# Batches of token products, lane marks shared out between engines, clearing in pieces, and a count that moves ahead of the last products

## The reference

```python
# layer 1: self-attention over the 1024 positions of an image
energy = einsum('bmi,bmj->bij', Wq @ x, Wk @ x)
y      = einsum('bcj,bij->bci', Wv @ x, softmax(energy))
x      = alpha * y + x
# layer 2: 16 proxies, a causal running sum over the tokens
prods = einsum('pd,bsd->bps', proxy, x)
y     = cumsum(prods[..., None] * x[:, None], axis=2)
out   = einsum('bps,bpsd->bsd', softmax(prods / 4, axis=1), y)
# layer 3: 8 experts, each token goes to the best two
top_w, top_idx = softmax(top_k(flat @ gate_w.T, 2))
out = sum_e combine[:, e] * (gelu(flat @ w1[e] + b1[e]) @ w2[e] + b2[e])
```

## Time and profile before

| | us |
|---|---|
| median of three runs | 832.53 (831.14 to 834.49) |
| profiled execution | 832.61 |
| its span, first to last instruction | 830.9 |
| stage A, B, C in that span | 241, 142, 448 |
| TensorE busy in A, B, C | 206, 84, 431 |

### The profile page before, as it was taken

The page is one execution under the profiler, slowest core; times in us unless marked ns, Lnnn a source line. Parts: engine busy times, 40 slices in busy tenths (PEclk is TensorE's granted clock), DMA queues, the critical chain, the costliest instruction groups (busy, mean ns, idle before and its releaser), DMA issues.

```text
span 830.9 us, 18535 instructions
## 1 busy us (share of the span) xinstructions
PE 721.0 (87%) x5410; PEld 682.9 (82%) x5411; DVE 503.1 (61%) x1152; ACT 310.9 (37%) x599; POOL 399.7 (48%) x462
## 2 busy tenths in 40 slices
PE   5898998989558667634999999999999999999993
PEld 4797897978546555424999999999999999999993
DVE  3787787877665989972545544554455445544551
ACT  2664854736324434212323332333223322332230
POOL 1564563734944323225355555555555555555233
PEclk9999999999968989855999999999999999999997
DMA  7569476493351212122175653754565445544222
GB/s 263 197 224 416 155 275 246 174 399 140 148 225 56 97 59 102 53 78 60 27 249 154 179 193 62 239 158 141 179 209 157 140 145 152 146 140 145 27 27 28
DMA packets 45868, 130.08 MB, mean 157 GB/s; under 512 B 5184, under 2 KB 35520, under 8 KB 41216
## 3 DMA queue, kind: packets, MB, share of 16 engines
q1 hardware_dynamic: 30560, 104.86, 33.4%
q0 software_dynamic: 13904, 19.45, 13.5%
q10 hardware_dynamic: 1360, 5.24, 1.6%
HBM read 186.80 MB, written 47.59 MB: 282 GB/s over the span
## 4 chain that ended last, share of the span: by engine, by line
PE 51%; issue 1%; DMA 1%; POOL 1%; DVE 0%; POOLq 0%; ACT 0%; DVEq 0%
PE ps_h L73 9%; PE ps_h L74 8%; PE ps_h L75 8%; PE ps_y L73 8%; PE ps_y L75 8%; PE ps_y L74 8%; PE ps_x L1545 2%; DMA out_tok<-y,to_row 0%; POOL out_tok L1425 0%; DMA x_rows<-normed,from_row 0%; POOLq L1348 0%; DVE yb L1505 0%; DVE xtl L1485 0%; DVE y L1512 0%; ACT xth L1450 0%
## 5 line engine op out<-in xcount | busy, mean ns | idle before, releaser
L1459 ACT ACTIVATE g<-ps_h,bias 128x256 f32<-128x256 f32 x288 | 120.8, 471 | 278.8 <-PE ps_h L75 278.8
L1425 POOL DMA_INDIRECT out_tok<-y,to_row x72 | 118.5, 1645 | 160.4 <-DVE y L1512 148.6
L73 PE MATMUL ps_h<-xth,wbuf 128*128 128x256 f32 x576 | 164.3, 285 | 3.3 <-issue 1.8
L73 PE MATMUL ps_y<-wbuf,gl 128*128 x576 | 164.5, 286 | 0.0
L74 PE MATMUL ps_h<-xtl,wbuf 128*128 128x256 f32 x576 | 164.1, 285 | 0.0
L75 PE MATMUL ps_h<-xth,wbuf 128*128 128x256 f32 x576 | 162.8, 283 | 0.0
L75 PE MATMUL ps_y<-wbuf,gh 128*128 x576 | 161.5, 280 | 0.0
L74 PE MATMUL ps_y<-wbuf,gh 128*128 x576 | 161.5, 280 | 0.0
L73 PEld LDWEIGHTS ps_h<-xth,wbuf 128*128 128x128 f32 x576 | 109.2, 190 | 3.9 <-issue 2.1
L75 PEld LDWEIGHTS ps_h<-xth,wbuf 128*128 128x128 f32 x576 | 110.8, 192 | 0.0
L74 PEld LDWEIGHTS ps_h<-xtl,wbuf 128*128 128x128 f32 x576 | 109.5, 190 | 0.0
(11 more groups left out here) (235 smaller groups left out, 1369.5 us busy)
## 6 DMA issues: line engine op xcount, KB each, us to landing
wbuf<-wsplit SPq DMA_DIRECT2D x71, 2048.0 KB, 7.3
wsplit<-wbuf SPq DMA_DIRECT2D x14, 2048.0 KB, 12.0
wraw<-in_w SPq DMA_DIRECT2D x16, 1024.0 KB, 7.6
raw<-in_x_ch ACTq DMA_DIRECT2D x5, 1024.0 KB, 10.1
normed<-x SPq DMA_DIRECT2D x8, 528.0 KB, 3.1
tok<-in_x_tok SPq DMA_DIRECT2D x1, 4096.0 KB, 16.6
out_tok<-tok SPq DMA_DIRECT2D x8, 512.0 KB, 3.7
x_rows<-normed,from_row POOLq DMA_INDIRECT x72, 3.2
```

The lines of the kernel that those rows point to most:

```text
L73: eng.matmul(out, ll, rh, start=first, stop=False)
L1425: pool.indirect_dma_start(out=out, out_offset=bass.IndirectOffsetOnAxis(ap=to_row[:, par, s:s + 1], axis=0), in_=y[:, par, s, :], in_offse ...
L1459: last = act.activation(g[:, f, :], ps_h[:, q, f % 2, :], ACT.Gelu_apprx_tanh, bias=bias1[:, bass.ds(e, 1), f:f + 1].rearrange("p a f -> p ...
```

## The change

1. The batches of token tiles become 16, 8, 4 and 4. The loop of stage A runs over two images, and images 2 and 3 are written out. In image 2 GpSimd makes the products of the first 16 tiles behind its second low part, VectorE does the first softmax half, and ScalarE the exponential at the image's end. In image 3 follow the batches of 8 and 4.
2. At the start of stage B, `prod` and `weight_t` are cleared in halves, TensorE's transposes wait for the two copies they read (`turn_in`) and not for all of `prepare`, and ScalarE evacuates the first transposes ahead of the first normalisation.
3. `mark_cells` makes one one-hot lane vector per pair (`lane`, eight instructions), and then the cells. GpSimd multiplies all eight with the tile's number in one instruction at the end of its body (`lanes_by_tile`), and ScalarE with the token's number in one (`lanes_by_part`). `record` waits for both and for the cells; the next chunk's lane marks wait until both have read `lane`.
4. The count of the experts' tokens stands ahead of the last chunk's record.

```diff
-BATCHES = ((0, NT - IT), (NT - IT, NT - REST), (NT - REST, NT))
+BATCHES = ((0, NT - 2 * IT), (NT - 2 * IT, NT - IT), (NT - IT, NT - REST), (NT - REST, NT))
+LAST = len(BATCHES) - 1
...
-            with eng.Fori(0, B - 1) as b:
+            with eng.Fori(0, B - 2) as b:
                 image(b, True)
+            image(B - 2, True)
             image(B - 1, False)
...
                                            wbuf[:, par, at:at + n].bitcast(F32), ALU.subtract).then_inc(w_lo, 1)
+                        if more and isinstance(b, int) and (par, part) == (0, 1):
+                            tok.products(pool, fixed, *BATCHES[0], 0)
                         if not more and par == 0:
-                            tok.products(pool, fixed, *BATCHES[part], part)
+                            tok.products(pool, fixed, *BATCHES[1 + part], 1 + part)
...
                         exp_tile(it + 2)
-                    if not more and it in (REST + 1, IT - 2):
-                        n = it // (IT - 2)
+                    if not more and it in (REST, IT - 2):
+                        n = 1 + it // (IT - 2)
                         tok.exponential(act, *BATCHES[n], n)
...
                     whole_qk(b + 1, 1)
+                if isinstance(b, int) and b == B - 2:
+                    tok.exponential(act, *BATCHES[0], 0)
...
-                    if it < B - 1:
-                        tok.mean_var(dve, it * IT, (it + 1) * IT, 0, it == B - 2)
-                    if it == REST:
+                    if more and it < 2:
+                        tok.mean_var(dve, it * IT, (it + 1) * IT, 0, it == 1)
+                    if more and it == IT - 2:
+                        tok.softmax_in(dve, *BATCHES[0], 0)
+                    if not more and it == 0:
                         tok.mean_var(dve, *BATCHES[1], 1)
-                        tok.softmax_in(dve, *BATCHES[0], 0)
-                    if it == IT - 2:
                         tok.softmax_out(dve, *BATCHES[0], 0)
+                    if not more and it == REST - 1:
                         tok.softmax_in(dve, *BATCHES[1], 1)
-                    if it == IT - 1:
+                    if not more and it == REST:
+                        tok.mean_var(dve, *BATCHES[2], 2)
+                    if not more and it == REST + 1:
                         tok.softmax_out(dve, *BATCHES[1], 1)
+                    if not more and it == IT - 2:
+                        tok.softmax_in(dve, *BATCHES[2], 2)
+                    if not more and it == IT - 1:
+                        tok.softmax_out(dve, *BATCHES[2], 2)
...
                 if isinstance(c, int):
-                    pool.wait_ge(tok.weights_d, 2 if c < REST else 3)
+                    pool.wait_ge(tok.weights_d, LAST if c < REST else LAST + 1)
                 else:
-                    pool.wait_ge(tok.weights_d, 3)
+                    pool.wait_ge(tok.weights_d, LAST + 1)
                 prods = chunk_of(tok.t[:, :, :], c)[:, :, C:C + NP]
                 pool.tensor_copy(prod_in[:, :, 0:NP], prods)
-                pool.tensor_copy(weight_in[:, :, 0:NP], chunk_of(tok.weights[:, :, :], c))
+                pool.tensor_copy(weight_in[:, :, 0:NP], chunk_of(tok.weights[:, :, :], c)).then_inc(turn_in, 1)
+                if isinstance(c, int) and c == 0:
+                    pool.wait_ge(zeroed, 1)
                 pool.tensor_copy(prod[:, par].rearrange("p (b n) -> p b n", b=B)[:, :, 0:NP], prods)
...
-            def next_tile(c):
-                wait_apart(pool, lane_d, done(c))
+            def lanes_by_tile(c, par):
+
+                pool.wait_ge(lane_d, done(c))
+                pool.wait_ge(rec_mm, done(c - 2))
+                pool.tensor_tensor(lane_tile[:, par].rearrange("p (k b) l -> p k b l", k=2),
+                                   lane[:, :, :].rearrange("p (k b) l -> p k b l", k=2),
+                                   tile_no[:, :].unsqueeze(1).unsqueeze(3).to_broadcast([P, 2, B, P]), ALU.mult).then_inc(lane_tile_d, 1)
+                wait_apart(pool, lane_tile_d, done(c))
                 pool.tensor_scalar(tile_no[:, :], tile_no[:, :], 1.0, None, ALU.add).then_inc(tile_d, 1)
+                wait_apart(pool, tile_d, done(c))
...
                 if exists(i - 1):
-                    next_tile(i - 1)
+                    lanes_by_tile(i - 1, 1 - par)
...
             pool.wait_ge(const0, 1)
-            pool.wait_ge(zeroed, 1)
             body(-2, 0)
+            pool.wait_ge(zeroed, 3)
             pool.memset(causal[:, :], 1.0).then_inc(const0, 1)
...
             pool.wait_ge(routing_set, 2)
-            tok.products(pool, fixed, *BATCHES[2], 2)
+            tok.products(pool, fixed, *BATCHES[LAST], LAST)
             for i in range(-1, 2):
...
         def _(act):
-            for s in (turned_d, x1_d, gexp_d, x2_d):
+            for s in (turned_d, x1_d, gexp_d, x2_d, lane_part_d):
                 act.sem_inc(s, CREDIT)
...
                     last = act.activation(weight_t[rows, par, b, :], ps_turn[rows, P:2 * P], ACT.Copy)
                 last.then_inc(turned_d, 1)
+
+            def lanes_by_part(c, par):
+
+                act.wait_ge(lane_d, done(c))
+                act.wait_ge(rec_mm, done(c - 2))
+                act.activation(lane_part[:, par], lane[:, :, :], ACT.Copy, scale=part_id[:, 0:1]).then_inc(lane_part_d, 1)
             def body(i, par):
...
                     evacuate_turned(i + 2, par)
+                if exists(i - 1):
+                    lanes_by_part(i - 1, 1 - par)
             act.wait_ge(zeroed, 2)
-            body(-2, 0)
+            evacuate_turned(0, 0)
+            first_norm(0, 0)
+            act.wait_ge(zeroed, 3)
             body(-1, 1)
-            tok.exponential(act, *BATCHES[2], 2)
+            tok.exponential(act, *BATCHES[LAST], LAST)
             for i in range(0, 2):
...
                 dve.wait_ge(spot_d, done(c))
+                dve.wait_ge(lane_tile_d, done(c - 1))
+                dve.wait_ge(lane_part_d, done(c - 1))
+                for kb in range(KB):
+                    last = dve.tensor_scalar(lane[:, kb, :], lane_id[:, :], spot[:, 0, kb:kb + 1], None, ALU.is_equal)
+                last.then_inc(lane_d, 1)
                 dve.wait_ge(rec_mm, done(c - 2))
...
                 last.then_inc(cell_d, 1)
-                wait_apart(dve, tile_d, done(c - 1))
-                for k in range(2):
-                    for b in range(B):
-                        mine = spot[:, 0, k * B + b:k * B + b + 1]
-                        dve.tensor_scalar(lane_tile[:, par, k * B + b, :], lane_id[:, :], mine, tile_no[:, b:b + 1],
-                                          ALU.is_equal, ALU.mult)
-                        last = dve.tensor_scalar(lane_part[:, par, k * B + b, :], lane_id[:, :], mine, part_id[:, 0:1],
-                                                 ALU.is_equal, ALU.mult)
-                last.then_inc(lane_d, 1)
+
             def mark(c, par):
...
-            dve.memset(prod[:, :, :], 0.0)
-            dve.memset(weight_t[:, :, :, :], 0.0).then_inc(zeroed, 1)
+            dve.memset(prod[:, 0], 0.0).then_inc(zeroed, 1)
+            dve.memset(weight_t[:, 0], 0.0).then_inc(zeroed, 1)
+            dve.memset(prod[:, 1], 0.0)
+            dve.memset(weight_t[:, 1], 0.0)
             dve.memset(state[:, :, :], 0.0)
...
             dve.memset(nothing[:, :], 0.0).then_inc(zeroed, 1)
-            tok.mean_var(dve, *BATCHES[2], 2)
+            tok.mean_var(dve, *BATCHES[LAST], LAST)
             dve.wait_ge(routing_set, 2)
             body(-1, 1)
-            tok.softmax_in(dve, *BATCHES[2], 2)
+            tok.softmax_in(dve, *BATCHES[LAST], LAST)
             body(0, 0)
-            tok.softmax_out(dve, *BATCHES[2], 2)
+            tok.softmax_out(dve, *BATCHES[LAST], LAST)
             body(1, 1)
...
             def turn(c):
-                pe.wait_ge(prep_d, done(c))
+                pe.wait_ge(turn_in, done(c))
                 pe.wait_ge(turned_d, done(c - 1))
                 if exists(c - 3):
...
                 pe.wait_ge(x1_d, done(c))
                 pe.wait_ge(state_d, done(c - 1))
+                pe.wait_ge(prep_d, done(c))
                 for b in range(B):
                     at = b * STRIDE - b * 2 * NP
...
-                pe.wait_ge(lane_d, done(c))
+                pe.wait_ge(lane_tile_d, done(c))
+                pe.wait_ge(lane_part_d, done(c))
                 pe.wait_ge(cell_d, done(c))
...
                     rank_choices(i - 1, 1 - par)
+                if isinstance(i, int) and i == CH + 1:
+                    pe.wait_ge(count_d, done(CH - 1))
+                    pe.wait_ge(attn_d, done(CH - 1))
+                    pe.matmul(ps_count, ones[:, :], counts_m[:, :], start=True, stop=True).then_inc(counted, 1)
                 if exists(i - 2):
...
-            pe.wait_ge(zeroed, 2)
-            pe.matmul(ps_rec[:, :], nothing[:, 0:P], nothing[:, :], start=True, stop=False)
             for i in range(-2, 2):
```

(6 more changed lines are left out.)

12 lines of the change are left out of this document (6 added, 6 removed).

## The result

| | us |
|---|---|
| before, median of 20 runs | 832.51 (830.9 to 834.84) |
| changed, median of 20 runs | 826.99 (824.5 to 833.09) |
| ratio | 0.9943, 95% interval 0.9925 to 0.9961 |
| profiled execution of the changed kernel, its span | 828.92, 827.1 |

By the medians the kernel became 5.5 us faster (4.7 by the ratio), where 13.1 were forecast. The time lies inside the forecast's whole range (808 to 828) and outside its own (814 to 825); the gain is less than half of the one forecast. Its runs also spread over 8.6 us, those of before over 3.9.

The account below looks back on a forecast made before the run. Bound by stage A's chain from statistics to TensorE, stage B's mask-to-record chain, then untouched TensorE-busy stage C. Gains 5.1 + 0.9 + 2.7 + 4.4 = 13.1 took 832.6 to 819.5 us; own range 814 to 825, whole range 808 to 828.

Parts of the forecast that it names:

- Stage A: New token batches shorten TensorE's wait in the last image: gain 9.9 less 1.8 and 3.0, 5.1 us, bounds 0 to 10.
- the bullet on the third low part: End of stage A: the third L359 ends near 227.6, its store lands at 235.7, before VectorE's last row; nothing charged.
- the 1.8 us of image 2: Stage A: charge before image 3 starts, for a sliding L359, held VectorE rows and added softmax steps; 0 to 3.
- the hole: Stage A, last image: TensorE's 10.37 us wait for a row of exponentials, forecast to shrink to 0.5.
- the held multiplication: Image 3: a VectorE softmax multiplication held beside L359 delays the row maximum; 3 us charged, 0 to 4.5.
- The forecast's own sign of being wrong: Forecast is wrong if stage A's last row ends later than 238 or GpSimd's product exceeds 2.6 us.
- Rival 2: Stage A gives its hole back: held VectorE rows in images 2 and 3 leave no gain there; 824.6 us, chance 0.12.
- The start of stage B: Clearing in pieces lets TensorE's second transpose go at 254.8, not 255.77; gain 0.9 us, bounds -0.9 to 1.0.
- The loop: Stage B: new lane marks start the record 0.4 to 0.45 us earlier per chunk; 2.7 us over six periods.
- the rival of flat cells: Stage B: cell marks are not held beside GpSimd's product, gaining 1.45 per chunk; 809.5 us, chance 0.13.
- The tail: End of stage B: the table starts right behind the last cells and covers the last record; gain 4.4, bounds 3 to 8.
- the rival of a long product: Stage B: GpSimd's product is longer, costing eight times each extra microsecond; 823 to 832 for 0.5 to 1.6; chance 0.17.

Follow-up runs that it names:

- the warm start: Changed kernel with 6 extra TensorE products of zeros behind stage B's first state products, ahead of the first outputs; 827.92 us, ratio 0.9931.
- a_only: Kernel before with only the new stage A batches (16, 8, 4, 4) and the unrolled image 2; 831.45 us, ratio 1.0005.
- warm_rec: Changed kernel with 10 extra TensorE products of zeros ahead of each record but the last; 819.89 us, ratio 0.9849.
- all_in: Changed kernel with softmax half after row 1, scalar-operand scale, lane products on ScalarE and VectorE, zeros ahead of records and first outputs; 803.04 us, ratio 0.9648.

## Why the prediction was wrong

- **Stage A is the step that failed**, and in it the bullet on the third low part. The first half of its working held: L359 of part 1 at 209.7 plus the 1.8 us of image 2, so 211.5, measured 212.05; the load issued at 216.73 (expected 214.4 + 1.8). Other terms were too small: the load took 7.0 us to ScalarE's row (216.73 to 223.73) and not 5.26 (the rows named give 5.28); the hole was 1.62 us and not 0.5; image 3 started 2.4 us late by its first low part (199.97 against 197.54) and not 1.8; the held multiplication took 3.14 us and the row maximum came 3.7 us late on top, for 3.0 expected. By its own numbers that leaves 10.37 - 1.62 - 2.4 - 3.7 = 2.6 us; the row of exponentials behind the hole came 3.2 us earlier (225.60, before 228.82).
- **The bullet on the third low part was wrong.** I asked only when its store would land, and charged nothing. The store did as forecast (issued at 229.75, waited for 6.9 us, so landed ahead of VectorE's last row). The rows that stood beside the third and the fourth low part are what it cost. From that row of exponentials to the end of stage A it is 17.1 us, and was 12.5: 4.6 us lost, through a scale of 2.82, a multiplication of 3.61 and TensorE's stand of 4.85. The rule was in the earlier trace rows, and in image 3 I used it for one instruction out of three. The runs bear this out: with the scale out of the way and the first multiplication still held, as the forecast had it, part 1 brings 4.8 us for the 5.1 forecast (822.08 against 826.85); with both moved it brings 8.7 (818.16), for 8.1 in the forecast's terms. The forecast's own sign of being wrong, a last row of stage A later than 238, came.
- **Rival 2** (824.6) came nearest of those whose mechanism the trace shows, and its idea is right: held rows ate the hole. But it put the loss down to image 2 and the first multiplication at their upper ends, 3 and 4.5 us; they were 2.4 and 3.7, and the rest of stage A's loss lay in the scale and the second multiplication, which it doesn't name. That five traces of this stage A end between 238.7 and 243.9 also says that the -1.4 of the table is one draw.
- **The start of stage B**: the 0.9 us was right for the transposes and wrong for the outputs. The clock, which I named in the bounds only (0.9 back, with -0.9 as the lowest), took 1.7 us; the warm start shows it. This term should have been -0.7, still inside its bounds.
- **The loop**: held cells, the longest 2.02 us, and a record 9.0 us behind the mask are what the forecast said, to a tenth of a microsecond; the rival of flat cells was wrong. But of the 0.45 us per period 0.27 went to the clock: record and scores took 4.48 us for 4.21, at a granted clock of 0.62 for 0.66. I had held the 4.21 constant while changing the idle stretch ahead of it.
- **The sentence from the Trainium skill** ("SBUF — State Buffer", section "Who interferes with whom"), that the two engines lock each other out for whole instructions, is borne out here for GpSimd's products: the longest cell mark is 2.02 us beside a GpSimd product of 1.89 to 2.05. It is not for GpSimd's power: the scale at 210.22 us of the kernel before takes 0.16 us inside a power of 4.20 us (L126 at 208.25). The same section of the Trainium skill says that a VectorE instruction with two SBUF inputs contends with a GpSimd one that reads SBUF; the scale of one element per partition, 2.82 us with two tensors and 0.215 at most with a scalar operand, agrees, but for the power.
- **The tail**: 4.65 for 4.4, by the steps given. No run has part 4, or part 2, by itself.
- **Stage C** takes 1.1 us longer from its first product (381.59, before 386.01) to the last; nothing was forecast. The granted clock over the first 14 us is 0.74 (first row, changed kernel) and was 0.79 (second row, before):

```profile
381.60:395.60 14.00, 12.15 (x73) 11.94 (x74) 4.87 (x7) 5.97 (x12) 8.97 (x12) 0.74 0.27 71
```

```profile
386.00:400.00 14.00, 12.14 (x78) 11.93 (x79) 4.80 (x7) 6.01 (x12) 8.91 (x10) 0.79 0.23 64
```

Over the twelve traces the two go together. Before, a_only and warm_rec have 0.79 or 0.80 and 431.4 to 431.6 us from the first product to the last, all_in has 0.75 and 431.8, and the other eight have 0.74 and 432.4 to 432.7. So the loss comes with parts 2 to 4, and it is gone with the zeros of warm_rec. That the clock is the cause is read from these traces; no run was made for it.
- **The slower side**: GpSimd's product took 1.9 to 2.05 us where 2.1 was put, and the rival of a long product had nothing in it.

## What to carry to other kernels

When work moves to another engine, list every instruction that will stand beside it in the new place, not only the ones that wait for it: a GpSimd addition of 4.6 us stops even a 128x1 product of two tensors until it ends (2.82 us here), and a held row can push the next one into the next hold. Where a tiny per-row product can take its second factor as a scalar operand, it is out of the lock at the price of 45 ns (0.204 us for 0.159). And where TensorE waits ahead of short critical products, compare the clock before shaving the wait: products of zeros in the idle stretch gave more (1.6 us per chunk) than the new marks (0.2).

## What was not expected of the hardware

- The two-tensor product of 128x1 takes up to 3.7 us behind a GpSimd addition, the same product with a scalar operand 0.215 us at most, in 32 rows. Inside a GpSimd power of 4.20 us the two-tensor product takes 0.16 us.
- The kernel with these holds spreads: 8.6 us over 20 executions, against 1.2 us over five once the two rows were moved (2.5 us over six with only the softmax half later, 3.7 over four with only the scalar operand).
- Ten TensorE products of zeros (2.3 us) ahead of a record keep the granted clock at 1.00 behind it, where it was 0.62. Without them the idle stretch is 3.3 us.
- The one-operation lane marks, 128 wide, are 0.16 us apart ((317.86 - 316.55)/8), hardly less than the cells of twice the width at 0.20.
